# A one-core kernel of four attention and feed-forward layers, run from a new table of step times

## The chip, the core and the metric

The kernel runs on one core of one Trainium2 chip. Its time is the device time of one execution in microseconds (us). Before the change three runs took 1153.56, 1161.57 and 1164.41 us; the median is 1161.57 us.

The core has a matrix engine (PE, with its weight loads shown apart as PEld), VectorE (DVE), ScalarE (ACT), GpSimd (POOL), and the queue of SyncE (SP), which issues nearly all the DMAs. Each engine runs its own list of instructions strictly in order and waits on semaphores for what the others make.

## What is computed

x is 8 batches of 256 tokens by 256 features, ctx is as large, and a mask is given for one layer. Cut to its core, with L = 0 to 3:

```python
x = x + L0_xattn(layernorm(x), ctx)        # 16 heads of 16, strictly causal
x = x + L0_ffn(layernorm(x))               # x @ sign(W)
x = x + L1_xattn(layernorm(x), ctx)        # causal
x = x + L1_ffn(layernorm(x))               # 16 routed experts, top 2, and 2 shared ones
x = x + L2_xattn(ctx, layernorm(x), mask)  # q, k and v are normalised too
x = x + L2_ffn(layernorm(x))               # ternary weights, activations rounded to 8 bits
x = x + L3_xattn(layernorm(x), ctx)        # no projections
x = x + L3_ffn(layernorm(x))               # 3 blocks of dequantised plus low-rank products
```

The ternary weights of layer 2 are scaled by the mean of their absolute values, so those weights (six pieces of 512 KB) are read once for the sum and once more for the rounding.

## The kernel before

The kernel is one long program for each engine. Work is cut into steps, and each step is a method that exists on one engine or on several. An item is (L, b), the attention of layer L for batch b; there are 32 items, and `ORDER` (line 74) fixes their sequence, which the change keeps. An item has 16 heads in 4 groups. For each head PE makes the scores for the row maximum (`maxima`), DVE reduces them (`reduce`), PE makes the scores again with the maximum taken off (`score`), ACT takes the exponential (`exp`), and for each group PE multiplies with the values (`values`).

Around the attention stand other steps. `ln` on DVE takes the moments of a layer norm, `ln_power` on POOL the inverse root, `apply` on ACT the normalised rows, `turn` and `turned` the transposed copy. `k_stack` and `q_stack` on SP write the bf16 parts of keys and queries, six DMAs each, into the layout that `maxima` reads. `project_in`, `projected` and `project_out` are the output projection. `fill` (12 DMAs on SP, 10 of 768 KB and 2 of 128 KB) presets the DRAM rows of the experts. `raw_load(c)` on SP reads one of six pieces of the ternary weights into the buffer that `mask_load` uses too, and `raw_sum(c)` on DVE sums it; `raw_load(c)` waits for `raw_sum(c-1)`, and `raw_load(0)` waits for `masks(1)`. `scatter` and `fetch` are POOL's indirect DMAs of the routed tokens, and `gather`, `tile_load`, `tile_up`, `tile_down`, `tile_store` handle one of 62 tiles of 128 routed rows, with its expert's weights, in rings of four buffers.

What sets the order is the table `AT` (line 115). Each of 378 lanes is a generator of steps that depend on each other, and `AT` holds for each lane the times of its steps, 5,036 in all, in tenths of a us. `program` (line 1202) sorts all these times and calls the steps in that order. So a time in the table is no wait: it fixes only the place of the step in the lists of its engines, SP's and POOL's among them. Correct results rest on semaphores alone. The same clock also picks the PSUM bank of a product (`claim`), out of the banks that the table takes to be free.

Before the program starts, SP issues nine DMAs: keys' input and x for batch 0, three weights, two small tables, then the same two inputs for batch 1.

`wait_score` (line 2589) makes POOL wait, before each of its 64 indirect DMAs, for the score that the table has last before it.

Of the kernel before, what the change touches and what calls it, by code (L numbers as in the profile page):

```python
# [8 lines left out]
ALU = mybir.AluOpType  # L9
# [89 lines left out]
class Signal:  # L99
# [8 lines left out]

    def at(self, key):

        return self.sem, self.unit * (self.known.get(key, 0) + 1)
# [3007 lines left out]
```

## Time and profile before

| | before |
|---|---|
| median of three runs | 1161.57 us |
| profiled execution, first to last instruction | 1166.1 us |
| PE busy | 1050.5 us, 90% of the span |
| DVE, ACT, POOL busy | 903.8, 804.5, 564.1 us |
| granted PE clock, mean | 0.970 |
| DMA moved | 140.03 MB |

The profiled execution's own time is its span of 1166.1 us; no other time was taken of it. In the profile a busy PE includes time in which it ran at the lower clock. Steps are recognised by line and tile: line 2010 is `exp`, 2247, 2255 and 2259 are `reduce`, 1580 is `maxima`, 1598 is `score`, 1688 is `values`, 2136 is `ln`, 2890 is a stack DMA, 2942 is `fill`, 2983 is `raw_load`, 2403 is `raw_sum`, 2935 is `mask_load` and 2194 is `masks`.

### The profile page before, as it was taken

To read this page: it belongs to the slowest core of one execution; us is meant where nothing else is said; L and a number is where in the kernel's file an instruction comes from. 1 tells how busy PE (TensorE), PEld (TensorE's weight loads), DVE (VectorE), ACT (ScalarE), POOL (GpSimd) and SP (SyncE) were. 2 spreads that over 40 slices of the span, in tenths; PEclk is the share of its full clock that TensorE was granted. 3 is DMA by queue.
4 is the path that set the end of the run, shared out by engine and by line. 5 is a ranking of instruction groups with operands and counts; after the bars stand their busy time and mean duration, and the time that the engine had idled before them with its cause. 6 is when DMAs were issued, how large, how long until landed. Compare 5 with 4: busy or idle time off the path is not lost.

```text
span 1166.1 us, 26103 instructions
## 1 busy us (share of the span) xinstructions
PE 1050.5 (90%) x8259; PEld 782.0 (67%) x8298; DVE 903.8 (78%) x3323; ACT 804.5 (69%) x1484; POOL 564.1 (48%) x1161
## 2 busy tenths in 40 slices
PE   7989999999999989898888898788898989989986
PEld 6667877777887866676666765556665665656664
DVE  3879887877564688898885588999997889887643
ACT  5757666566674555566565667656989899998962
POOL 7232364655122365577830125766455454545443
PEclk9999999999999998999999999979999999999997
DMA  7985322325667643412258864232132222222000
GB/s 239 312 284 143 92 74 56 91 74 173 203 181 210 200 127 82 136 47 84 81 185 262 249 184 147 84 92 76 39 100 73 73 55 56 83 64 55 1 19 19
DMA packets 102327, 140.03 MB, mean 120 GB/s; under 512 B 12336, under 2 KB 79792, under 8 KB 102192
## 3 DMA queue, kind: packets, MB, share of 16 engines
q1 hardware_dynamic: 98688, 129.57, 38.0%
q0 software_dynamic: 3072, 8.39, 2.3%
q8 instruction: 69, 1.13, 0.4%
q14 instruction: 66, 0.54, 0.1%
q10 hardware_dynamic: 432, 0.39, 0.1%
HBM read 65.43 MB, written 22.54 MB: 75 GB/s over the span
## 4 chain that ended last, share of the span: by engine, by line
PE 40%; DVE 18%; ACT 15%; DMA 8%; issue 7%; SPq 5%; POOL 5%; another core or an unknown queue 1%; DVEq 0%; POOLq 0%; ACTq 0%
PE ps L1559 9%; PE ps L1688 4%; ACT probs L2010 4%; PE ps L1580 4%; PE ps L1598 4%; SPq L2890 3%; PE ps L1781 3%; PE ps L1552 3%; PE ps L1566 2%; ACT q_st L2027 2%; DVE ps L2247 2%; DMA w<-in_expert 2%; PE ps L1601 2%; DVE ps L2255 2%; PE ps L1748 1%
## 5 line engine op out<-in xcount | busy, mean ns | idle before, releaser
L2010 ACT ACTIVATE probs<-ps 128x384 f32<-128x384 f32 (+1 forms) x512 | 260.2, 545 | 91.4 <-PE ps L1601 46.4
L1580 PE MATMUL ps<-k_st,q_st 96*128 96x256 bf16 (+1 forms) x1024 | 172.4, 266 | 26.8 <-DVE neg_max L2247 10.3
L1598 PE MATMUL ps<-q_st,k_st 104*128 104x256 bf16 (+1 forms) x1024 | 178.0, 263 | 16.8 <-ACT probs L2010 12.3
L2027 ACT ACTIVATE q_st<-ps 8x1024 bf16<-8x1024 f32 x128 | 129.9, 1016 | 24.4 <-PE ps L1669 21.8
L1580 PEld LDWEIGHTS ps<-k_st,q_st 96*128 96x128 bf16 x1024 | 86.8, 100 | 79.1 <-DVE neg_max L2247 19.1
L2247 DVE CUSTOM_DVE_ANT_0 ps<-ps,diag_s 128x128 f32<-128x128 f32 (+1 forms) x384 | 123.3, 358 | 20.9 <-PE ps L1580 18.7
L1598 PEld LDWEIGHTS ps<-q_st,k_st 104*128 104x128 bf16 x1024 | 90.7, 99 | 61.7 <-issue 19.5
L1688 PE MATMUL ps<-probs,v 128*32 128x256 f32 (+1 forms) x2048 | 126.0, 365 | 2.0 <-ACT probs L2010 1.9
L2576 POOL TENSOR_SCALAR var_eps<-mv 128x2 f32<-128x2 f32 (+1 forms) x115 | 27.8, 242 | 185.2 <-DVE mv L2139 180.1
L2255 DVE CUSTOM_DVE_ANT_0 ps<-ps,mask_s 128x256 f32<-128x256 f32 x256 | 101.4, 452 | 6.2 <-PE ps L1580 5.8
L2658 POOL CAST parts<-qf 128x512 bf16<-128x512 f32 x64 | 40.5, 633 | 100.3 <-DVE qf L2166 44.7
L1688 PEld LDWEIGHTS ps<-probs,v 128*32 128x32 f32 x2048 | 55.0, 110 | 49.9 <-issue 25.8
L2259 DVE TENSOR_REDUCE neg_max<-ps 128x2 f32<-128x512 f32 x128 | 82.5, 680 | 5.4 <-PE ps L1580 2.9
L2581 POOL TENSOR_TENSOR rstd<-var_eps,neg_half 128x2 f32<-128x2 f32 (+1 forms) x115 | 84.4, 734 | 0.6
L2660 POOL TENSOR_TENSOR parts<-qf,parts 128x512 bf16<-128x512 f32 x64 | 75.0, 1173 | 5.2
L1559 PE MATMUL ps<-w,xn_t 128*128 128x256 f32 x296 | 74.1, 394 | 1.8 <-ACT xn_t L1906 1.2
L1959 ACT ACTIVATE xn<-x,shift,rstd 128x256 f32<-128x256 f32 x112 | 64.0, 633 | 16.2 <-POOL shift L2586 12.1
L1781 PE MATMUL ps<-ring,w 128*128 128x128 f32 x496 | 67.1, 281 | 6.5 <-DMA w<-in_expert 4.0
L2247 DVE DVE_READ_ACCUMULATOR2_ANT neg_max<- 128x1 f32 x512 | 72.5, 142 | 0.0
L1601 PE MATMUL ps<-diag_t,ident_b 128*128 128x256 bf16 x256 | 71.0, 278 | 0.0
L1781 PEld LDWEIGHTS ps<-ring,w 128*128 128x128 f32 x496 | 61.6, 193 | 12.1 <-issue 7.6
L1559 PEld LDWEIGHTS ps<-w,xn_t 128*128 128x128 f32 x296 | 54.7, 195 | 13.5 <-issue 6.8
(275 smaller groups left out, 2548.9 us busy)
## 6 DMA issues: line engine op xcount, KB each, us to landing
k_st<-parts SPq DMA_DIRECT2D x192, 128.0 KB
q_st<-parts SPq DMA_DIRECT2D x189, 128.0 KB, 2.8
w<-in_expert SPq DMA_DIRECT2D x62, 384.0 KB, 4.2
x_rows<-wo SPq DMA_DIRECT2D x10, 768.0 KB, 10.9
ctx_t<-in_ctx_t SPq DMA_DIRECT2D x16, 256.0 KB, 3.0
ring<-x_rows SPq DMA_DIRECT2D x31, 128.0 KB, 3.3
y_rows<-ring SPq DMA_DIRECT2D x31, 128.0 KB, 3.7
xn_t<-x_rows SPq DMA_DIRECT2D x31, 128.0 KB, 4.0
```

The lines of the kernel that those rows point to most:

```text
L1559: last = mm(t[:, a * D:(a + 1) * D], act_t[:, kt, a * P:(a + 1) * P], weight[:, kt, :], start=kt == 0, stop=kt == KT - 1)
L1580: last = mm(t[:, c0:c0 + n], head(q_st, r, h, KROWS, j * P, P), head(k_st, r, h, KROWS, 0, n), start=j == 0 or not by_pe, stop=not by_pe, ...
L1598: last = mm(t[:, j * S:j * S + n], head(k_st, r, h, KALL, j * P, P), head(q_st, r, h, KALL, skip, n), start=j == 0 or L == 3, stop=L == 3, ...
L1601: last = mm(t.rearrange("p (j t) -> p j t", j=SJ)[:, :, 0:P], ident_b[:, :], diag_t[:, L, :, :], start=False, stop=True, skip_group_check= ...
L1688: last = mm(t[h4 * DPAD:(h4 + 1) * DPAD, skip:S], v[:, r, j, hg * HPG + h4, :], probs[:, (hg % 2) * HPG + h4, j * S:(j + 1) * S - skip], s ...
L1781: last = mm(t[:, n * P:(n + 1) * P], expert[:, i % RING, c0:c0 + INNER_E], x_tile_t[:, i % 2, kt * P:(kt + 1) * P], start=kt == 0, stop=kt ...
L2010: nc.scalar.activation(probs[:, (hg % 2) * HPG + h4, 0:width], tile_of(key)[:, 0:width], ACT.Exp, scale=SCALE).then_inc(*tile_drained(key))
L2027: nc.scalar.activation(out, tile_of(key)[KROWS:KALL, 0:S].unsqueeze(1).to_broadcast([2 * HPG, HPG, S]), ACT.Copy).then_inc(*tile_drained(key))
L2247: last = V.tensor_tensor_reduce(some, some, diag_s[:, n0:n0 + j * step + 1:step, :], -1.0, -NEG, ALU.add, ALU.min, neg_max[:, hg, h4, j:j ...
L2255: last = V.tensor_tensor_reduce(some, some, mask_s[:, b % 2, j, :], -1.0, -NEG, ALU.add, ALU.min, neg_max[:, hg, h4, j:j + 1])
L2259: V.tensor_reduce(neg_max[:, hg, h4, :], tile_of(key).rearrange("p (j t) -> p j t", j=SJ), AX.X, ALU.max, negate=True).then_inc(*tile_drai ...
L2581: G.tensor_tensor(rstd[:, kind, tiles], var_eps[:, kind, tiles], neg_half[:, 0:SJ if a is None else 1], ALU.pow).then_inc(*ln_rstd.step((p ...
```

## The change

The table is replaced by another one with the same lanes and the same number of steps in each; its times are in hundredths of a us. No step changes its engine. `wait_score` goes. `sum_inv` gets two halves. Waits are written out where a buffer is used again: in `projected`, `quantised_copy`, `down_copy`, `normalise`, `load_batch` and `tile_load`.

```diff
@@ AT, first lines of four lanes (scores, fills, early, constants)
-    (287, 292, 303, 305, 322, 325, 339, 342, 370, 373, 386, 391, 416, 419, 432, 435, 456, 459, 470, 473, 496, 498, 509, 512,
...
-    (307, 313, 319, 336, 342, 348, 516, 543, 549, 555, 561, 567),
-    (168, 178, 184, 189, 195, 200, 205, 522),
-    (8, 65, 162, 219),
...
+    (3165, 3195, 3423, 3475, 3608, 3651, 3826, 3855, 3976, 4025, 4161, 4190, 4280, 4376, 4500, 4528, 5049, 5080, 5368, 5396,
...
+    (3322, 3366, 3405, 3444, 3483, 3522, 3561, 3600, 3639, 3678, 3717, 3756),
+    (1865, 1948, 2177, 2216, 2255, 2294, 2333, 2494),
+    (0, 866, 1624, 2382),
...
@@ program
-        clock[0] = t / 10
+        clock[0] = t / 100
@@ build
-        sum_inv = sb("sum_inv", [P, SJ, 2 * HPG])
+        sum_inv = sb("sum_inv", [P, 2, SJ, 2 * HPG])
@@ ACT
                 def projected(L, b):
+                    n = SLOT[L, b] - 1
+                    while n >= 0 and ORDER[n][0] == 3:
+                        n -= 1
+                    if n >= 0:
+                        wait_filled(act, ("wo", *ORDER[n]))
                     drain(("op", L, b), o_t[:, :, :])
                 def quantised_copy(b):
+                    if b:
+                        for T in range((b - 1) * SJ, b * SJ):
+                            for c in range(2):
+                                wait_filled(act, ("hu", T, c))
                 def down_copy(T):
+                    if T >= SJ:
+                        wait_filled(act, ("hd", T - SJ))
@@ DVE, normalise
+                    if SLOT[L, b]:
+                        wait_drained(dve, ("ot", *ORDER[SLOT[L, b] - 1], pair))
@@ POOL
-            def wait_score():
-
-                n = sum(10 * clock[0] > t for t in AT[0])
-                if n:
-                    L, b = ORDER[(n - 1) // H]
-                    wait_filled(pool, ("s", L, b, *divmod((n - 1) % H, HPG)))
...
-                    wait_score()
@@ SP, load_batch
-                if L == 0 and b >= 4:
-                    wait_filled(sp, ("v", 1, b - 4))
+                read = b - 4 if L == 0 else b + 4
+                if L == 0 and b >= 4 or L == 2 and b < 4:
+                    for what in ("k", "v"):
+                        for layer in range(2):
+                            wait_filled(sp, (what, layer, read))
@@ SP, tile_load
-                        wait_filled(sp, ("logit", LAST))
-                        wait_filled(sp, ("ed", LAST))
+                        for b in (B - 2, LAST):
+                            wait_filled(sp, ("logit", b))
+                            wait_filled(sp, ("ed", b))
```

Decoded with the lanes' generators, some entries of the two tables read as follows (us in the table, not measured):

| step | engine | before | after |
|---|---|---|---|
| load(0,3), inputs of batch 3 | SP | 22.0 | 0.0 |
| ln of batch 3 | DVE | 49.9 | 3.6 |
| ln of batch 0 | DVE | 3.7 | 4.5 |
| mask_load(0), masks(0) | SP, DVE | 32.5, 49.2 | 0.8, 5.4 |
| mask_load(1), masks(1) | SP, DVE | 53.2, 62.0 | 6.2, 10.1 |
| k_stack, q_stack of item (0,0) | SP | 10.1, 14.9 | 14.9, 19.9 |
| first maxima, first exp | PE, ACT | 19.9, 29.5 | 24.2, 33.6 |
| 12 fills | SP | 30.7 to 34.8 and 51.6 to 56.7 | 33.2 to 37.6 |
| raw_load(0), raw_sum(0) | SP, DVE | 62.9, 69.0 | 10.9, 15.6 |
| raw_load(1), raw_sum(1) | SP, DVE | 70.3, 77.7 | 24.5, 30.1 |
| raw_load(2), raw_sum(2) | SP, DVE | 80.1, 84.0 | 38.0, 43.2 |
| exp 49 of the 512 in sequence | ACT | 93.2 | 96.3 |
| exp 177 | ACT | 318.4 | 286.3 |
| last exp of layers 0 and 1 (exp 256) | ACT | 497.3 | 433.2 |
| exp 257 | ACT | 499.2 | 540.8 |
| exp 292, exp 293 | ACT | 580.9, 610.5 | 616.3, 616.8 |
| exp 353 | ACT | 763.0 | 729.8 |
| tile_load, first to last of tiles 0 to 30 | SP | 269.3 to 378.1 | 332.9 to 454.2 |
| tile_load, first to last of tiles 31 to 61 | SP | 563.1 to 633.1 | 490.2 to 580.9 |
| last exp | ACT | 1057.1 | 1032.1 |
| half_store(0), half_store(1), the last step | SP | 1106.5, 1107.5 | 1074.7, 1075.6 |

## Rows read from the trace of the kernel before

**Rows 1.** The page: span, busy time by engine, and PE's clock in 40 slices.

```profile
span 1166.1 us, 26103 instructions
PE 1050.5 (90%) x8259; PEld 782.0 (67%) x8298; DVE 903.8 (78%) x3323; ACT 804.5 (69%) x1484; POOL 564.1 (48%) x1161
PEclk9999999999999998999999999979999999999997
```

**Rows 2.** Busy time in six stretches: us, engines with counts, clock, DMA share, GB/s.

```profile
0.00:80.00 80.00, 65.89 (x517) 51.34 (x518) 51.61 (x240) 50.09 (x85) 34.77 (x82) 0.95 0.92 292
80.00:320.00 240.00, 230.76 (x2031) 184.39 (x2030) 189.82 (x909) 155.97 (x308) 111.09 (x258) 0.99 0.39 113
320.00:560.00 240.00, 218.82 (x1733) 174.09 (x1738) 181.67 (x759) 144.13 (x305) 125.30 (x261) 0.96 0.46 134
560.00:800.00 240.00, 208.50 (x1531) 148.17 (x1550) 194.46 (x633) 151.12 (x299) 107.27 (x194) 0.96 0.52 154
800.00:1120.00 320.00, 291.78 (x2306) 197.94 (x2320) 265.86 (x733) 288.58 (x458) 164.16 (x330) 0.99 0.22 61
```

**Rows 3.** Line 2010 alone in stretches from 0: ACT busy (count), clock, DMA.

```profile
0.00:102.80 102.80, 21.22 (x48) 0.95 0.82 257
0.00:332.40 332.40, 79.51 (x176) 0.98 0.53 160
0.00:527.20 527.20, 115.81 (x256) 0.97 0.51 151
0.00:817.90 817.90, 171.72 (x353) 0.96 0.51 149
```

**Rows 4.** The same for the stretch in which no exponential starts.

```profile
0.00:615.90 615.90, 135.75 (x292) 0.97 0.50 147
0.00:647.50 647.50, 136.24 (x292) 0.97 0.51 152
```

**Rows 5.** Timeline of SP at the end: start, us, what.

```profile
1162.23 2.04 SPq L3018 DMA_DIRECT2D out<-x  x2
```

**Rows 6.** Timeline of SP, DVE and ACT at the start, idle before in brackets.

```profile
4.56 0.66 SPq L2854 DMA_DIRECT2D x<-in_x  x1
4.20 0.75 DVE L2136 BATCH_NORM_STATS2 bn<-x 128x6 f32<-128x256 f32 x2 [4.20 <-DMA x<-in_x]
11.29 0.75 DVE L2136 BATCH_NORM_STATS2 bn<-x 128x6 f32<-128x256 f32 x2 [0.59 <-DMA x<-in_x]
21.90 0.30 DVE L2247 CUSTOM_DVE_ANT_0 ps<-ps,diag_s 128x128 f32<-128x128 f32 x1 [1.51 <-PE ps L1580]
32.42 1.02 ACT L2010 ACTIVATE probs<-ps 128x384 f32<-128x384 f32 x2 [1.48 <-PE ps L1601]
```

**Rows 7.** Timeline of SP, DVE and PE around the first `raw_load`.

```profile
58.85 3.55 SPq L2942 DMA_DIRECT2D x_rows<-wo  x5
68.35 0.33 SPq L2983 DMA_DIRECT2D mask_raw<-in_wq_gate  x1
77.54 1.22 DVE L2403 TENSOR_REDUCE wsum<-mask_raw 128x1 f32<-128x1024 f32 x1 [4.32 <-DMA mask_raw<-in_wq_gate]
79.53 0.87 PE L1566 MATMUL ps<-ident,o_tok 128*128 128x128 f32 x3 [4.22 <-DVE o_tok L2285]
```

**Rows 8.** DMA issues: name, count, KB each, median us from issue to landing.

```profile
x_rows<-wo SPq DMA_DIRECT2D x10, 768.0 KB, 10.9
...
mask_raw<-in_wq_up SPq DMA_DIRECT2D x4, 512.0 KB, 3.7
```

**Rows 9.** The stretch of the first six fills: columns as in rows 2.

```profile
33.60:51.80 18.20, 16.74 (x182) 12.57 (x181) 14.91 (x83) 14.39 (x26) 3.53 (x4) 0.97 1.02 342
```

**Rows 10.** Waits: who waited for whom, us in total, times, longest.

```profile
ACT o_t L1906 <- PE ps L1566: 8.9, 4, 4.6
SPq L2864 <- PE ps L1559: 11.9, 3, 8.2
POOL ring L2816 <- PE ps L1601: 5.1, 3, 1.8
POOL xn_t L2816 <- PE ps L1598: 4.2, 3, 2.2
```

More of the change, by code:

```diff
@@ L107, in step, with drain @@
         return self.sem, self.unit
+    def drain(self, key):
+        return self.sem, self.unit
     def at(self, key):
@@ L1429, in tile_drained @@
             new_drain_at[key] = clock[0] + DRAIN
-            return drained[bank_of[key]].sem, 1
+            return drained[bank_of[key]].drain(key)
         def wait_filled(eng, key):
@@ L2280, in normalise @@
                     wait_filled(dve, key)
+                    if SLOT[L, b]:
+                        wait_drained(dve, ("ot", *ORDER[SLOT[L, b] - 1], pair))
+                    inv = sum_inv[:, pair, :, :]
                     t = tile_of(key).rearrange("p (a h e) -> p a h e", a=SJ, e=DPAD)
-                    V.reciprocal(sum_inv[:, :, :], t[:, :, :, DH]).then_inc(*inverted.step((L, b, pair)))
+                    V.reciprocal(inv, t[:, :, :, DH]).then_inc(*inverted.step((L, b, pair)))
                     dve.wait_ge(*inverted.at((L, b, pair)))
                     out = o_tok[:, r, :, pair * 2 * HPG * DH:(pair + 1) * 2 * HPG * DH].rearrange("p a (h d) -> p a h d", d=DH)
-                    V.tensor_tensor(out, t[:, :, :, 0:DH], sum_inv[:, :, :].unsqueeze(3).to_broadcast([P, SJ, 2 * HPG, DH]), ALU.mult).then_inc(
+                    V.tensor_tensor(out, t[:, :, :, 0:DH], inv.unsqueeze(3).to_broadcast([P, SJ, 2 * HPG, DH]), ALU.mult).then_inc(
                         *tile_drained(key))
@@ L2814, in fetch @@
                             pool.wait_ge(*y_out[i % RING].at(i))
-                    wait_score()
                     G.indirect_dma_start(y_in(b, n), None, y_rows[g],
@@ L2856, in load_batch @@
             def load_batch(L, b):
-                if L == 0 and b >= 4:
-                    wait_filled(sp, ("v", 1, b - 4))
+                read = b - 4 if L == 0 else b + 4
[3 more added lines that the diff above has]
+                            wait_filled(sp, (what, layer, read))
                 if L == 2:
-                    if b < 4:
-                        wait_filled(sp, ("v", 1, b + 4))
-                    else:
+                    if b >= 4:
+                        for what in ("k", "v"):
+                            wait_filled(sp, (what, 2, b - 4))
                         sp.wait_ge(*part_rest.at(("k", 3, b - 4)))
```

1077 rows, old and new, of the table AT are left out of this document.

## The prediction

> **What bounds the kernel now.** I read the page first. PE is busy for 1050.5 of 1166.1 us [rows 1], so no order of the same steps can save more than PE's idle 115.6 us and what the lower clock costs. The mean granted clock of 0.970 puts that at 0.03 x 1166.1 = 35 us or less. By stretch [rows 2] the idle time is 14.1 of the first 80 us, 9.2 of the next 240, 31.5 of the 240 from 560 and 28.2 of the 320 from 800. DVE is the second engine, busy for 194.5 of 240 us from 560 to 800.
>
> Then I asked how well the old table foretold the run. The exponentials can be counted: 48 have run at 102.8 us, 176 at 332.4, 256 at 527.2 and 352 (the count of 353 has one table load in it) at 817.9 [rows 3]; the next one starts at once in each case. The old table puts these at 93.2, 318.4, 499.2 and 763.0. So the run is behind its table by 9.6, 14.0, 28.0 and 54.9 us, and by 55.7 at half_store(0), which starts at 1162.23 for a table time of 1106.5 [rows 5]. The last 350 us add under 1 us: there the table is as good as a measurement. What the table misses is 2.9 us at the first exponential against 29.5 in the table [rows 6], 6.7 up to 102.8, and 46 between 102.8 and 1162.
>
> **The sum's frame.** The new table's last step stands at 1075.6, the old one's at 1107.5. The span ends at 1166.1, that is 2.9 us after table time plus 55.7. So the new span is 1075.6 + 2.9 + lag = 1078.5 + lag, and the question is the lag. I take a table time for nothing but this: a place from which measured lateness is counted.
>
> **Lag at the start: 7 us.** DVE's first step becomes the ln of batch 3, whose x is now the eleventh DMA. The ninth is issued at 4.56 and lands at 11.29, with DVE waiting for it [rows 6]; two more of 256 KB behind it, 0.9 us each at the 292 GB/s of the first 80 us [rows 2], put this one at about 13. Before, DVE began at 4.20. Behind stand the ln of batch 0, masks(0), only then SP's mask_load(1), which takes 3 us or more (512 KB take 3.7, [rows 8]), masks(1) and then the first k_rest: about 20 us. POOL, from the ln of batch 0 at 15, has some 13 us of steps in its list up to the end of q_low of item (0,0), and q_stack lands 3 us later, near 31. The table wants the first maxima at 24.2: 7 us late, against 2.9 before. Bounds: 4 and 10.
>
> **Lag from the raw sums: 21 us.** This is the largest cost. The 12 fills (7.9 MiB, 8.1 MB) stood in two lots of six; now they stand in one row on SP, and raw_load(2) is right behind them. The trace of before has this in small: raw_load(0), issued at 68.35 behind the second lot, reached DVE at 77.54, 9.2 us against 3.7 for a lone one [rows 7, 8]. DVE idled 4.32 us, PE then 4.22, since only two PSUM banks hold maxima [rows 7]. Transfers land nearly in the order of issue: a fill takes 10.9 us in the median [rows 8]. In the new list SP has, from 28 us on, 4.5 MB of weights and inputs, two stacks of 0.8 MB and then the fills. The first part, 6.1 MB, lands by about 49 us at 292 GB/s. The fills need 8.1 MB at 342 GB/s [rows 9] = 24 us, or 19 at the 430 that a stretch of pure fills might reach (my upper guess). raw_load(2), 1.5 us behind them, then lands between 69.5 and 74.5, and raw_sum(2) ends 1.2 us later [rows 7]. The table ends it at 44.4. So the lag is 26 to 31 there, and I take 28. raw_sum(1), also behind 2 MB of weights, is a step of 2 us on the way and is contained in it. Behind raw_sum(2) on DVE stand normalise of (0,0) and all row maxima; behind raw_load(3) on SP, which waits for raw_sum(2), stand the stacks of item (0,2). PE is planned nearly without gaps from there to 433, so little of it is won back. Bounds for the whole start: 10 (no more than before had) and 33 (two us on top of the upper value).
>
> **Lag from 100 us on: 23 us.** Before it was 46. Part of that was a table that priced PE's steps too low: with each kind of PE step at the distance which the table usually leaves to the next step (a third up the sorted distances), the old table's PE steps sum to 967 us and the new one's to 993. Those 26 us of work are already in the new table's 1075.6, so they no longer come as lag. The other 20 are lower clock (at most 30 of the 35 us lie behind 102.8) and late transfers; I keep them. The long stall at the start adds 3: after its 4.22 us stall PE's clock was down for a while [rows 7], and the mean of the first 80 us is 0.95 [rows 2]. Bounds: 8 (a denser PE keeps its clock) and 46 (everything comes again).
>
> **The edits in code: 0.** The new waits name work that PE has long done in either table: the wo before a project_in, hu before quantised, hd by 20.9 us or more before the next down_turn. Their cover is PE's own order. ACT's wait in projected was 8.9 us in all and is for the turn that follows wo [rows 10]. The wait in normalise is for DVE's own earlier step; without cover each costs one semaphore turn. SP's waits in load_batch name k and v of layers 0 and 1; the latest of them is v of layer 1, which it waited for before (11.9 us, [rows 10]). wait_score held POOL 5.1 and 4.2 us in front of two groups of fetches [rows 10]; nothing late hangs on them now, so its removal gains 0, at best 5.
>
> **Sum.** 28 + 23 = 51; span 1078.5 + 51 = 1129.5 us. The profiled execution lies 4.5 us above the median of 1161.57, so I forecast 1125 us, 3.1% less. Where the gain would come from is PE's idle time between 320 and 800 and after; where it is lost is the first 80 us.
>
> **Rival A, the front costs little.** If a late transfer does not have to wait for those issued before it, raw_load(2) lands 4 to 5 us after issue and the early lag is 11: 1078.5 + 11 + 23 - 4.5 = 1108. Against it stand the 9.2 us of rows 7; for it, that the same DMA engines serve all. With the later bound of 8 it would be 1093. The Trainium skill (DMA: Bandwidth & Descriptors, section Queues, rings and completion order) says of transfers of one issuing engine that completion is not in the order of issue, only the start on each DMA engine. By that sentence's first half alone this rival would hold, by its second the forecast does; the 9.2 us agree with the second. Chance 0.2.
>
> **Rival B, the gain is eaten.** The later lag comes in full: 28 + 46 = 74, and the table has a stretch of 107.6 us without exponentials (433.2 to 540.8), in which tiles, ternary weights and layer 2's projections must fill PE. Before, such a stretch of 29.6 us in the table (580.9 to 610.5) took 31.8 [rows 4], 7% more; that is 8 us here. Sum 1078.5 + 82 - 4.5 = 1156. For it: DVE, at 194.5 of 240 us, is packed tighter in the new table between 560 and 800. Against: the last 350 us of before, where DVE was as dense (265.9 of 320, [rows 2]) and nothing was lost. Chance 0.19.
>
> **Rival C, slower.** The queue at the front is the mechanism, at a higher price. With the 54 us of rival B's later part, 1173 (1% more than before) is reached at an early lag of 45. That needs the fills and what stands before them to drain in 15 us more than at 342 GB/s, so at about 210, and raw_load(3) and the stacks of (0,2) late by as much. At an early lag of 50 it is 1178 us. The first stretch moved 292 GB/s in the mean [rows 2], which speaks against. Chance 0.09.
>
> **Numbers.** Forecast case 0.52, A 0.2, B 0.19, C 0.09. About 1% is what a measurement of this kernel can tell from no change (its three runs lie 0.9% apart). Faster by over 1% (below 1150): the forecast case, A and a fifth of B, 0.75. Within 1%: 0.16. Slower: 0.09. The range: 1078.5 + 10 + 8 - 4.5 = 1092 below and, with both upper bounds, 1078.5 + 33 + 46 - 4.5 = 1153 above; I take 1094 to 1160, to hold half of B above its sum too.
>
> **What would show it.** DVE's first moments at 12 to 13 us and not 4; the first exponential at 40 us (3 either way); one idle stretch of DVE in front of its third line 2403 of 10 us or more, ended by the DMA of the raw weights, and PE idle behind it; exponential 49 at about 124 us; from there on a lag that grows by 20 to 25 us to the end. PE's idle time from 320 to 800 falls from the 52.7 us of before to some 25. If exponential 49 comes before 110, the front is priced too high; if the lag after it grows by over 40, the second half is where I am wrong.

## The result and the profile after

The changed kernel takes 1167.54 us (median of 16 runs, 1163.5 to 1172.4), the kernel before 1160.58 beside it (16 runs). The ratio is 1.0062, 95% interval 1.0040 to 1.0085: 7 us or 0.6% slower. I had forecast 1125 us, faster by 3.1%, with a range that ended at 1160; the kernel lies above it. The outcome within 1% of before had been given a chance of 0.16.

The page of the kernel after, for [rows 1]:

```profile
span 1167.5 us, 26206 instructions
...
PE 1041.5 (89%) x8298; PEld 783.1 (67%) x8298; DVE 899.4 (77%) x3323; ACT 805.8 (69%) x1486; POOL 561.6 (48%) x1161
...
PEclk7779999999999899999999998999999999999998
```

Busy time of every engine is within 1% of before. PE's idle time grew from 115.6 to 126.0 us. The three slices of 7 at the left of the clock row are new. The stretches of [rows 2], after:

```profile
0.00:80.00 80.00, 41.45 (x264) 31.81 (x264) 30.04 (x118) 31.01 (x49) 29.94 (x71) 0.79 0.79 270
80.00:320.00 240.00, 230.36 (x2062) 180.39 (x2062) 194.26 (x961) 160.82 (x306) 95.61 (x197) 0.98 0.32 90
320.00:560.00 240.00, 225.88 (x1835) 188.99 (x1835) 167.72 (x735) 134.66 (x306) 119.11 (x311) 0.98 0.54 165
560.00:800.00 240.00, 214.83 (x1607) 153.73 (x1608) 206.03 (x699) 168.95 (x329) 133.40 (x223) 0.96 0.55 157
```

Both halves of the result are in these rows. In the first 80 us PE did 264 matmuls where it did 517 before, and idled for 38.5 us instead of 14.1. From 320 to 800 it idles for 14.1 + 25.2 = 39.3 us instead of 52.7. A gain stands behind, a loss in front.

The count of exponentials (line 2038 now), for [rows 3]; 48 have run when the next one starts at 133.8, 176 at 328.1, 256 at 601.5:

```profile
0.00:133.70 133.70, 21.43 (x48) 0.85 0.62 203
0.00:328.00 328.00, 79.13 (x176) 0.94 0.43 132
0.00:486.80 486.80, 114.89 (x256) 0.95 0.46 142
0.00:601.40 601.40, 115.38 (x256) 0.95 0.51 155
```

The new table has these at 96.2 (96.25, rounded up in the table of steps), 286.3 and 540.8, so the run is 37.6, 41.8 and 60.7 us behind it, and 89.0 at half_store(0), which starts at 1163.71 for a table time of 1074.7 (for [rows 5]):

```profile
1163.71 2.04 SPq L3055 DMA_DIRECT2D out<-x  x2
```

Exponential 49 is the best place to cut the run, since nearly the same work lies in front of it in both tables (408 of 423 steps are the same). Columns as in [rows 2], first the kernel before, then after, each with its part up to exponential 49 and its tail:

```profile
0.00:102.90 102.90, 88.47 (x716) 68.85 (x717) 72.09 (x324) 66.13 (x115) 43.95 (x97) 0.95 0.82 256
102.90:1166.10 1063.20, 962.06 (x7546) 713.13 (x7583) 831.71 (x3001) 738.33 (x1371) 520.19 (x1064) 0.97 0.37 107
```

```profile
0.00:133.80 133.80, 90.71 (x698) 69.32 (x698) 74.71 (x333) 64.88 (x112) 44.76 (x97) 0.85 0.62 203
133.80:1167.50 1033.70, 950.84 (x7600) 713.77 (x7600) 824.67 (x2991) 740.94 (x1375) 516.88 (x1064) 0.98 0.38 109
```

The front became 30.9 us longer, of which 28.7 is PE idle time (43.1 against 14.4). The tail became 29.5 us shorter: 18.2 less idle, 11.2 less busy, the latter with the clock at 0.98 instead of 0.97. The old table's tail is 1014.3 us and the new one's 979.4, a promise of 34.9.

What fills the front, timelines of SP, PE, ACT and DVE of the kernel after (for [rows 6, 7]):

```profile
13.35 0.75 DVE L2175 BATCH_NORM_STATS2 bn<-x 128x6 f32<-128x256 f32 x2 [13.35 <-DMA x<-in_x]
38.04 0.80 PE L1608 MATMUL ps<-k_st,q_st 96*128 96x128 bf16 x4 [5.15 <-DMA q_st<-parts]
40.33 3.81 SPq L2926 DMA_DIRECT2D k_st<-parts  x6
55.61 0.60 ACT L1976 ACTIVATE parts<-ps 128x512 bf16<-128x512 f32 x1 [8.85 <-issue]
56.10 0.87 ACT L2038 ACTIVATE probs<-ps 128x384 f32<-128x384 f32 x2
49.92 10.52 SPq L2978 DMA_DIRECT2D x_rows<-wo  x12
60.48 19.22 SPq L3020 DMA_DIRECT2D mask_raw<-in_wq_up  x2
78.13 1.22 DVE L2445 TENSOR_REDUCE wsum<-mask_raw 128x1 f32<-128x1024 f32 x1 [11.73 <-DMA mask_raw<-in_wq_up]
80.67 1.13 PE L1608 MATMUL ps<-k_st,q_st 96*128 96x128 bf16 x4 [10.08 <-DVE neg_max L2286]
```

Two stalls are in these rows. The first exponential waits on ACT behind `k_hi` of item (0,2) (line 1976), which idles ACT for 8.85 us; by the code it waits until the stack DMAs of item (0,1) have landed, and these were issued from 40.33 on, behind the weights. The profile names no releaser here (`<-issue`). The other thing that the step waits for, POOL's splits of item (0,1), had ended by 43.1, so the stacks are what is left; the trace of e4_front below names them. The second is the forecast one: `raw_load(2)` issued at 60.48 right behind twelve fills, landed for 78.13, DVE idle for 11.73 us and PE for 10.08 behind it.

### The profile page after: what moved, and what is told of

Its sections match the earlier page's. It is cut to its first block, busy times and chain, and to the rows that moved or that the text cites. A ratio compares the mean times of both kernels' runs of the same rounds, so it can differ in the third digit from the quotient of the medians.

```text
span 1167.5 us, 26206 instructions
## 1 busy us (share of the span) xinstructions
PE 1041.5 (89%) x8298; PEld 783.1 (67%) x8298; DVE 899.4 (77%) x3323; ACT 805.8 (69%) x1486; POOL 561.6 (48%) x1161
## 4 chain that ended last, share of the span: by engine, by line
PE 45%; DVE 27%; ACT 8%; DMA 6%; SPq 6%; issue 6%; POOL 2%; DVEq 0%; another core or an unknown queue 0%; POOLq 0%; ACTq 0%
PE ps L1587 10%; PE ps L1716 5%; PE ps L1608 4%; PE ps L1626 4%; DVE ps L2294 4%; PE ps L1809 4%; PE ps L1580 3%; DVE ps L2286 3%; DVE bn L2175 3%; SPq L2926 3%; PE ps L1594 3%; ACT probs L2038 2%; DMA mask_raw<-in_wq_up 2%; DVE neg_max L2298 2%; PE ps L1816 2%
## 5 line engine op out<-in xcount | busy, mean ns | idle before, releaser
L2618 POOL TENSOR_SCALAR var_eps<-mv 128x2 f32<-128x2 f32 (+1 forms) x115 | 28.8, 250 | 216.9 <-DVE mv L2178 211.0
L2693 POOL CAST parts<-qf 128x512 bf16<-128x512 f32 x64 | 39.7, 621 | 119.9 <-DVE qf L2205 52.7
L1716 PEld LDWEIGHTS ps<-probs,v 128*32 128x32 f32 x2048 | 54.5, 110 | 48.8 <-issue 24.2
L1587 PE MATMUL ps<-w,xn_t 128*128 128x256 f32 x296 | 71.6, 385 | 3.6 <-ACT xn_t L1934 1.3
L1809 PEld LDWEIGHTS ps<-ring,w 128*128 128x128 f32 x496 | 64.9, 199 | 9.2 <-issue 4.5
L1587 PE MATMUL ps<-w,ctx_t 128*128 128x256 f32 x256 | 64.1, 395 | 0.2 <-DVE ring L2515 0.2
```

What stands on the lines that cost most here:

```text
L1587: last = mm(t[:, a * D:(a + 1) * D], act_t[:, kt, a * P:(a + 1) * P], weight[:, kt, :], start=kt == 0, stop=kt == KT - 1)
L1716: last = mm(t[h4 * DPAD:(h4 + 1) * DPAD, skip:S], v[:, r, j, hg * HPG + h4, :], probs[:, (hg % 2) * HPG + h4, j * S:(j + 1) * S - skip], s ...
L1809: last = mm(t[:, n * P:(n + 1) * P], expert[:, i % RING, c0:c0 + INNER_E], x_tile_t[:, i % 2, kt * P:(kt + 1) * P], start=kt == 0, stop=kt ...
```

## The experiments

All times below are medians, and ratios are to the kernel before, run beside each; its own median was 1157.14 to 1161.10 us from one set of runs to the next, so different runs are compared by their ratios. Exponential 49 and spans come from each run's profiled execution. Steps are named and given their table times in us.

**The code edits alone (e1_edits).** The old table in the new code.

```diff
-AT = (new table)
+AT = (old table, each time x 10)
```

> The old table (times multiplied by ten, so the same order) in the new code. My theory, the forecast's: the code edits cost 0, so 1160 us, within 0.3% of before, and exponential 49 at 102.8 us. Rival: the new waits are part of the 50 us by which the new kernel falls behind its table after 134 us; then this kernel is slower than before, by 5 to 27 us, and by the same stretch it lags the old table by more than 55 us at the end.

Measured: 1153.54 us, ratio 0.9975 (0.9947 to 1.0003). The edits cost nothing that can be measured. Its profiled execution taught more:

```profile
0.00:105.00 105.00, 88.80 (x715) 69.19 (x716) 72.98 (x324) 66.05 (x114) 43.70 (x97) 0.95 0.80 251
105.00:1146.60 1041.60, 948.94 (x7546) 704.86 (x7583) 830.06 (x3001) 739.39 (x1371) 521.00 (x1064) 0.99 0.38 109
```

The same order and the same work as before has a tail of 1041.6 us here and of 1063.2 in the execution that I had read. 13.1 of the 21.6 are PE busy time, at a clock of 0.99 against 0.97. The old table has 1014.3 us for the tail, so its later lag, 48.9 us by span in the execution that I had read (the forecast's 46 counts to half_store(0)), is 27.3 in this one.

That this execution is quick is not the edits' doing: at 1148.37 us it is the quickest of its twelve (1148.37 to 1159.73). The 35 executions of the kernel before that ran beside it spread by 16 us, and with the clock: those with a mean granted clock of 0.984 took 1147.94 and 1149.71 us, those with 0.971 took 1157.23, 1161.43 and 1163.56. A profiled execution at 0.970, as I had read, and one at 0.984, as here, are near the two ends.

**Raw sums later (e2_raws), batch 3 later (e3_ln3), the whole front as before (e4_front).** All three on the new kernel:

```diff
 # e2_raws
-raw_load(2..5) 38.0 44.5 53.4 65.3   raw_sum(2..5) 43.2 49.1 64.0 70.0   raw_total 90.6   round_load(0) 101.3
+raw_load(2..5) 62.0 72.3 83.0 100.4  raw_sum(2..5) 68.5 77.9 91.2 111.1  raw_total 157.9  round_load(0) 165.0
 # e3_ln3
-load(0,3) 0.0   ln 3.6   ln_power 4.7   apply 29.3  turn 32.2  turned 38.6
+load(0,3) 23.4  ln 49.9  ln_power 51.0  apply 54.8  turn 60.2  turned 61.1
 # e4_front: e3_ln3 and
-masks(0), masks(1) 5.4 10.1   fill(0..11) 33.2 .. 37.6                raw_load(0) 10.9
+masks(0), masks(1) 49.2 62.0  fill(0..5) 30.7 ..  fill(6..11) 51.6 ..  raw_load(0) 62.9
   (the other raw loads and sums at 70.3 .. 111.1, raw_total 157.9, round_load(0) 165.0)
```

> The new kernel, but pieces 2 to 5 of the raw weights are loaded and summed later (table times 62 to 111 us instead of 38 to 70; sum of all and first round load behind them). Fills and everything else stay. Theory: the 11.7 us for which DVE stood in front of raw_sum(2) go, the first exponential stays at 56 us, exponential 49 comes about 12 us earlier (121 to 123 us), and the whole is about 1155 us. Rival: the queue of 12 fills itself is the cost, because the stacks of item (0,2) and their rows stand behind it as well; then exponential 49 stays within 3 us of 133.8 and the time within 3 us of 1167.

> The new kernel, but batch 3's input is loaded and normalised later, at the old table's place (load at 23.4, ln at 49.9, its later steps behind). Theory: DVE starts at 4 us and not at 13.4, the first exponential comes 6 to 9 us earlier (47 to 50 us), raw_sum(2) by the same 6 to 9, and the whole is 1159 to 1162. Rival: the masks and the raw weights ahead of the first stack hold the start as well; then the first exponential moves by under 3 us and the time stays within 3 us of 1167.

> The new kernel, but batch 3's load and ln, both masks, all fills, all raw loads and sums and the total are put at the old table's places (fills in two lots again). Theory: the front alone costs 28 us, PE is packed from there on and gives nothing back; exponential 49 at 106 to 110 us instead of 133.8 and the whole at 1137 to 1144 us, faster than both kernels. Rival: the early lateness is slack that a later wait would have used anyway (the tiles, the 108 us without exponentials); then exponential 49 comes early as well, but the lag after it grows by 65 to 78 instead of 50 and the time stays above 1155.

| | exponential 1 | exponential 49 | ratio to before |
|---|---|---|---|
| after | 56.1 | 133.8 | 1.0062 (1.0040 to 1.0085) |
| e2_raws | 55.8 | 127.5 | 1.0033 (1.0005 to 1.0061) |
| e3_ln3 | 49.2 | 126.9 | 1.0045 (1.0019 to 1.0071) |
| e4_front | 43.7 | 114.7 | 0.9956 (0.9928 to 0.9983) |

Each step moves exponential 49 in the direction foretold. e3_ln3 met its numbers for the front (DVE starts at 4.14, and the third raw sum, at 71.69, is 6.4 us earlier), e2_raws gave half (6.3 us for 12), between its two expectations. For the whole both had been expected to give more: 1.0033 and 1.0045 are 1164 and 1165 us beside a before of 1160, foretold were 1155 and 1159 to 1162. Alone they are worth 0.2 to 0.3% with intervals that overlap those of the kernel after; only both together, with masks and fills, make it faster than before. e4_front was 8 to 15 us slower than foretold by its median of 1151.67 us, 11 to 18 by its ratio, and the chain of waits of that run up to its first exponential shows why:

```profile
31.80 11.34 DMA k_st<-parts
43.21 0.60 ACT parts L1799
43.81 0.39 ACT probs L1861
```

The last of the k stack DMAs of item (0,1) took 11.34 us to land, with the weights issued in front of it, and `k_hi(0,2)` stands in front of the first exponential in the new table (31.8 against 33.6), while the old one has it 6.4 us behind.

**That wait alone (e7_khi).** e4_front with the splits of item (0,2) moved behind the first exponentials.

```diff
-k_hi(0,2) 31.8  q_hi(0,2) 36.3  (k_rest, k_low, q_rest, q_low 37.1 to 39.8)
+k_hi(0,2) 42.0  q_hi(0,2) 45.0  (k_rest, k_low, q_rest, q_low 43.0 to 46.5; q_stack 45.8 -> 48.6)
```

> The kernel with all of the front moved (e4_front), and beside that ScalarE's k_hi and q_hi of item (0,2) with the split steps behind them stand 9 to 10 us later in the table, behind the first exponentials. Theory: in e4_front k_hi(0,2) stands in front of the first exponential and waits 11.3 us for the stack DMAs of item (0,1), which are behind 3 MB of weights; the first exponential comes at 33 to 37 us instead of 43.7, exponential 49 at 106 to 110 instead of 114.7, and the time is 5 to 8 us less than e4_front's 1151.7. Rival: the maxima of the next groups need the same stacks; then the first exponential comes early, but exponential 49 stays within 2 us of 114.7 and so does the time.

Measured: 1149.87 us, ratio 0.9901 (0.9869 to 0.9934); first exponential at 36.97, no longer behind a DMA, exponential 49 at 110.0. The 4.7 us came through in the trace; the ratio moved by 0.55% (6 us), with intervals that overlap a little. The rival said exponential 49 would stay, and it did not.

**The fills alone (e9_fills).** The new kernel, only the fills moved.

```diff
-fill(0..11) 33.2 .. 37.6 (0.4 apart)
+fill(0..11) 85.0 .. 178.5 (8.5 apart)
```

> The new kernel, but the 12 fills alone are moved, from the table times 33 to 38 us to 85 to 179 us, one at a time. Masks, batch 3 and all raw loads and sums stay where the new table has them. Theory: raw_sum(2) came 35 us late because 8.1 MB of fills stand right in front of its load; without them it comes at 58 to 64 us instead of 78.1, exponential 49 at 116 to 121 us instead of 133.8, and the time is 13 to 18 us less than the new kernel's 1167.5. Rival: the weights and stacks in front hold the raw load as much; then raw_sum(2) comes after 70 us and the time is within 6 us of 1167.5.

Measured: 1155.21 us, ratio 0.9956 (0.9934 to 0.9977), so 12.3 us less than after, just under the foretold 13 to 18. The third raw sum, DVE timeline:

```profile
66.65 1.21 DVE L2268 TENSOR_REDUCE wsum<-mask_raw 128x1 f32<-128x1024 f32 x1
```

It starts at 66.65, not 78.13 (foretold 58 to 64), and waits for no DMA. Exponential 49 comes at 122.3 instead of 133.8 (foretold 116 to 121), and what was gained by then (11.5 us) is there at the end. The first exponential stays at 55.4: that stall is not the fills'. This one move of twelve instructions is worth more than the whole loss of the change.

**Old front, new tail, and the reverse (e5_oldfront, e6_newfront).** In the new code, the 423 steps up to exponential 49 in one table's order, all others in the other's.

```diff
 # e5_oldfront: time of a step
-T_new
+T_old + 3.0 if T_old < 93.2 else T_new   (the 15 only the new front has: 96 to 114 us; raw_total 157.9, raw_scale 162, round_load(0) 165)
 # e6_newfront
+T_new if T_new < 96.2 else T_old + 3.0   (the 15 only the old front has: 96.2 to 97.2 us)
```

> The new code and the new table, but the first 423 steps (all up to exponential 49) stand in the old table's order; the ten steps that only the new table has in that part follow directly behind. Theory: front and tail add. The old front puts exponential 49 at 103 to 106 us, the new tail from there takes its 1034 us, so 1135 to 1140 us, 2% less than before. Rival: the tail was quick only because everything behind the long stall was ready (weights, fills, stacks); then the tail takes 1045 to 1060 us and the time is above 1148.

> The reverse: the new table's order up to exponential 49, the old table's order behind it. Theory: exponential 49 at 132 to 135 us and the old tail of 1045 to 1063 us, so 1180 to 1195 us, slower than both kernels by 2%. Rival: the old tail takes up part of the lateness, since its table leaves PE more idle time; then the time is 1160 to 1175.

e5_oldfront: 1147.99 us, ratio 0.9883 (0.9860 to 0.9906). e6_newfront: 1211.06 us, ratio 1.0429 (1.0407 to 1.0451). The two profiles, cut at exponential 49:

```profile
0.00:105.00 105.00, 88.85 (x716) 69.73 (x717) 72.13 (x324) 66.14 (x114) 43.71 (x97) 0.93 0.78 251
105.00:1145.10 1040.10, 947.42 (x7545) 709.76 (x7583) 827.86 (x3001) 740.97 (x1373) 516.86 (x1064) 0.98 0.38 109
```

```profile
0.00:132.80 132.80, 89.84 (x700) 68.48 (x701) 75.06 (x333) 65.19 (x112) 44.77 (x97) 0.86 0.64 205
132.80:1206.00 1073.20, 963.59 (x7561) 713.79 (x7598) 827.39 (x2991) 740.79 (x1373) 520.61 (x1064) 0.97 0.36 105
```

The first measures the new order behind exponential 49: 1.17% or 13.6 us better than the old one, with the old front. The new front then costs 1.0062 - 0.9883 = 1.8% or 21 us, of 28.8 us that exponential 49 comes later: the tail behind the long stall is 1033.7 us and that behind the short front 1040.1. So 6 to 8 us seem to come back, as the rival had it in kind but not in size; the ratios are sure to some 4 us, and the tails are of one execution each, so this is likely and not shown. It would account for most of the 8 us by which e5_oldfront missed my 1140. The reverse, above both expectations, is spoilt by its seam: item (1,0), its steps squeezed together with the 15 that had been put off, took 32 us for 15 exponentials where the kernel before took 17. With these 15 us taken off, some 35 of its 50 us are left for the new front with the old tail; no more than that can be read from it.

**Fills and raw sums spread (e8_spread).** On e5_oldfront.

```diff
-fill(0..11) in two lots at 34 and 55 to 60   raw_sum(0..5) 72 .. 114
+fill(0..11) 42.0 .. 168.5, 11.5 apart        raw_sum(0..5) 92 .. 212, 24 apart
   (raw_load(0..5) 12 in front of each sum; raw_total 232, raw_scale 236, round_load(0) 240)
```

> e5_oldfront with the 12 fills spread over the table times 42 to 169 us and the raw loads and sums over 80 to 212 us, each alone on the queue. Theory: what is left of the front's lateness (9.7 us at exponential 49, most of it behind raw sums and fills) is the queue again; exponential 49 at 99 to 102 us and the time 2 to 5 us under e5_oldfront's. Rival: no transfer is late in the old front any more and the rest is PE and DVE work; then it is within 1 us of e5_oldfront, or 1 to 3 us slower, since raw sums now stand in the dense part of DVE.

Measured: 1140.49 us, ratio 0.9819 (0.9796 to 0.9843). This beats both kernels: 1.8% under before and, by 0.9819 / 1.0062, 2.4% under after. It gains 0.64% on e5_oldfront, 7.4 us, more than foretold:

```profile
0.00:99.70 99.70, 86.92 (x716) 67.78 (x717) 70.34 (x325) 66.17 (x114) 44.18 (x97) 0.97 0.69 209
99.70:1137.80 1038.10, 944.95 (x7545) 710.40 (x7583) 828.59 (x2999) 741.23 (x1373) 516.92 (x1064) 0.98 0.39 115
```

5.3 us of it lie in front of exponential 49. Fills and raw pieces moved together here, so their shares are not known.

**What the tail is short of (e10_dve2, e11_dve01, e12_half).** On e8_spread, in `reduce` on DVE:

```diff
 # e10_dve2 (condition L == 2), e11_dve01 (L < 2 and not one of the first three items)
+                    if L == 2:
+                        V.tensor_reduce(probe[:, h:h + 1], diag_s[:, 0:2, :].rearrange("p n k -> p (n k)"), AX.X, ALU.max)
                     wait_filled(dve, key)
 # e12_half
-   tile_of(key).rearrange("p (j t) -> p j t", j=SJ),
+   tile_of(key).rearrange("p (j t) -> p j t", j=SJ)[:, :, 0:P],
```

> e8_spread with one more VectorE reduction (128x256 bf16, a result that nothing reads) in front of each of layer 2's 128 row maxima: 128 of some 0.3 us, about 40 us of DVE between 570 and 980 us. It asks what the new tail is short of. Theory: there PE waits mostly for DVE, which is busy 209 of 231 us from 569 on, so this costs over half of what it adds, 20 us or more. Rival: PE alone sets the pace and DVE has room; then it costs under 8 us.

> e8_spread with the same reduction in front of the 208 row maxima of layers 0 and 1 from item (1,0) on: 208 of some 0.3 us, about 65 us of DVE between 97 and 460 us. Theory: DVE is busy for only 349 of 469 us from exponential 49 to layer 2, so PE sets the pace and this costs under 15 us. Rival: only two PSUM banks hold maxima, so each us before a reduce is a us for PE whatever DVE's idle time; then it costs 30 us or more.

> e8_spread, but layer 3's 128 row maxima on VectorE are taken over only half of the keys (128x256 instead of 128x512, 0.68 us each in e8_spread; the maximum is then not the true one, the rest of the work is as before). That takes some 0.27 us off each, 35 us of DVE in all, after 720 us. Theory: the added reductions passed on three quarters of their DVE time to the whole, so the tail is short of DVE as much as of PE, and taking time away gives back half or more: 15 to 26 us less than e8_spread. Rival: PE's idle time there is of other origin and DVE was only just in time; added DVE work costs, removed work gains under 6 us.

| | DVE busy | time | ratio to before | against e8_spread |
|---|---|---|---|---|
| e8_spread | 898.9 | 1140.49 | 0.9819 (0.9796 to 0.9843) | |
| e10_dve2 | 933.0 | 1166.98 | 1.0057 (1.0031 to 1.0082) | +34.1 busy, +2.4%, 27.6 us |
| e11_dve01 | 955.7 | 1179.24 | 1.0174 (1.0144 to 1.0204) | +56.8 busy, +3.6%, 41 us |
| e12_half | 868.9 | 1131.26 | 0.9744 (0.9708 to 0.9780) | -30.0 busy, -0.8%, 9 us |

(Last column: difference of the ratios x 1160 us; by the intervals of the ratios each is sure to 4 or 5 us.) The added reduction stands in front of the wait for PE's scores, so it could have filled time in which DVE waits. Added DVE time still comes through at 81% and 73%. For e10_dve2 that is my theory. For e11_dve01 it is the rival's side: I had said under 15 us, because DVE was idle for a quarter of that stretch, and it cost 41. Less DVE time gave back 30% (9 us, 4 to 14 by the intervals), between the two expectations. The profiled execution of e12_half, the slowest of its six, has a span of 1137.8 us, the same as that of e8_spread; in it DVE's waits for PE in front of the shortened maxima grew from 10.6 to 21.8 us. PE's waits in the stretch of layer 2, first in e8_spread (570 to 960 us), then in e10_dve2 (570 to 980): us in total, times, longest.

```profile
PE ps L1431 <- DVE neg_max L2121: 4.4, 4, 3.2
PE ps L1431 <- DVE neg_max L2117: 4.3, 8, 1.4
PE ps L1449 <- ACT probs L1861: 4.1, 3, 2.3
```

```profile
PE ps L1432 <- DVE neg_max L2120: 15.2, 31, 1.7
PE ps L1521 <- DVE max_parts L2137: 6.2, 13, 1.9
```

Eight waits of half a us in front of the maxima (L1431, L1432) become 31. Of the 27.4 us by which the span grew, 16.8 are PE idle time and 10.6 PE busy time (1042.5 against 1031.9), at a granted clock of 0.976 against 0.981. My reading is that PE, DVE and the two banks between them run in step: a delay of either is felt, a relief of one only until the other is next. It is not shown, because time was added in layers 0 to 2 and taken away in layer 3, and no run did both to the same layer.

## Why the prediction was wrong, step by step

My forecast put exponential 49 at 124 us and the tail at 1129.5 - 124.2 = 1005.3 us. They are 133.8 and 1033.7. So of the 42.5 us between 1125 and 1167.54, 9.6 are the front and 28.4 the tail. The remaining 4.5 are what I took off because the execution I had read lay above its median; the new kernel's profiled span, 1167.5, is its median.

**The front's place and mechanism: right, and too small.** DVE's first moments came at 13.35 (12 to 13 foretold) and the idle stretch of 10 us or more before the third raw sum was there (11.73), with PE idle behind it. e9_fills shows the fills as the cause of 11.5 us of it.

**"Lag at the start: 7 us": failed.** It was 22.5, the first exponential at 56.1 and not 40. I had walked DVE's and POOL's lists up to the first maxima and put these at 31; they came at 38.04, after a wait for q_st. ACT's list I had not walked. There `k_hi(0,2)` waits for DMAs issued from 40.33 to 44 behind the weights; it idled ACT for 8.85 us, and e7_khi shows 6.7 us for its place in e4_front. Batch 3's load and ln, which I did price, are worth 6.9 us at the first exponential (e3_ln3). For the sum only the part counts that makes SP's list late, because the landing of raw_load(2) holds DVE whenever the first exponential comes. Batch 3 is such a part: with it moved SP issues its load of batch 2 at 23.55 and not at 30.88, and its 6.9 us are there at exponential 49 too (e3_ln3). When the fills are gone, 26.0 us of lag are left at exponential 49 (e9_fills).

**"Lag from the raw sums: 21 us", to 28 in all: mis-sized.** raw_sum(2) ended at 79.35 where I had 72.4, and 2.7 us more were lost up to exponential 49; the 37.6 are 4.6 over my upper bound of 33. The rate was right:

```profile
30.00:78.10 48.10, 25.44 (x202) 17.86 (x200) 20.61 (x93) 25.87 (x41) 14.63 (x18) 0.82 0.95 336
```

336 GB/s over the whole queue, where I had 292 for its first part and 342 for the fills. But the weights went out from 30.88 and not from 28: a queue that is full hands its late start on, 2.9 of the 7.0 us. Most of the other 4 are a miscount of bytes: by the sizes of its DMAs, SP's list from 30.88 up to raw_load(2) holds 15.9 MB and not 14.7. The weights, inputs and first stack in it are 5.6 MB where I had 4.5, and 1.2 MB at 336 GB/s are 3.4 us.

**"Lag from 100 us on: 23 us": failed, the largest error.** It was 1033.7 - 979.4 = 54.3 by span, against 1063.2 - 1014.3 = 48.9 before. The credit of 26 us for a table that prices PE's steps higher was an artefact. Distances between neighbours in a table are, as I now read them, work plus the gap that the planner leaves, so a sum of them is no price of the work. The two rows of each tail tell: PE is busy for 962.1 us in the old tail, 950.8 in the new one, the same work within 1.2% (948.9 in e1_edits' tail, which makes it 0.2%), so the old table's 1014.3 left PE some 52 us idle and the new one's 979.4 some 29, and the real idle time was 101.1 and 82.9. These two executions idle PE by about 50 us more than their tables say. Nor is that a constant of the kernel: the later lag is 49 to 61 us in the eight profiled executions that have the new tail (after, e2, e3, e4, e5, e7, e8, e9), and 27.3 and 48.9 in the two that have the old one. The new table's lag is the larger one, where I had made it the smaller. Rival B had this part nearly right: 46 + 8 = 54, against 51.4 counted to half_store(0). PE's idle time from 320 to 800 fell by 13.4 us, to 39.3, and not to some 25.

Within it, the 8 us for the stretch without exponentials measured 7.1 (a lag of 53.6 at 486.8 us, 60.7 at 601.5). The rest grew in small pieces, from 328 to 487 and from 602 to 839 most. Another 10 came behind 839 (a lag of 78.6 at exponential 370, 89.0 at half_store(0)); from exponential 370 on the old table's had stood still (55.2 to 55.7), and I had called a table as good as a measurement there. That DVE is part of its cause e10_dve2 and e11_dve01 show; how much of the 50 us is DVE's, the lower clock's or transfers' is open, and e12_half speaks against DVE as the whole. The step that failed is known, the cause of the lag itself stays open.

**The old lag of 46 was itself one draw.** The same order had 27.3 against 48.9 in e1_edits. I had one execution, at a granted clock of 0.970, and took it as the kernel's.

**The code edits: 0, right** (ratio 0.9975, an interval that holds 1).

**Rival C, slower, is what the sum came near,** from below and with rival B on the other side (1167.5 between 1156 and 1173): it asked for an early lag of 45 and a later one of 54; the later was there (51.4 at half_store(0)) and the early one was 37.6, which gives slower by 0.6% and not by 1%. I had called it unlikely because it needed 210 GB/s. It came near with no low rate at all, by a later lag that I had credited away. **Rival A** fell: raw_load(2) landed 17.6 us after its issue. The Trainium skill (DMA: Bandwidth & Descriptors, Queues, rings and completion order) says that each DMA engine takes turns between the queues for which it has work. The three q stack DMAs that ACT issued on its own queue at 27.93 landed in 2.5 us in the median, but SP's queue was nearly empty then, so no run here shows whether another queue would have spared the stacks the 11.34 us.

## What to carry to other kernels

Bulk transfers with no reader for 100 us (fills, second copies of weights) belong one by one between the urgent ones, never in a row in front of them: spreading the fills gave 12 us here in the bad order, and fills and raw pieces together 7 in the good one. When an order is judged, walk the list of every engine up to the first useful step, ask of each step that waits for a DMA what was queued ahead of that DMA, and start a queue's count at the real time of its first issue. And compare two plans by measured busy time at the same milestones; a lag read from one execution here was uncertain by 20 us, and its mean granted clock hints at which end it lies.

## What the runs showed of the hardware

An idle front goes with a lower clock. Up to exponential 49 the granted clock is 0.85 after, with PE idle for 43.1 us, and 0.95 before, with 14.4; both are a mix of its levels of 1.2 and 2.4 GHz. PE is busy for 2.2 us more there than before, for 18 matmuls fewer. In the stretch in which ACT waited for the stack and PE with it, the granted clock was 0.70, with PE busy for 1.06 of 7.0 us:

```profile
50.70:57.70 7.00, 1.06 (x7) 0.80 (x8) 0.12 (x2) 2.07 (x4) 0.00 (x0) 0.70 1.10 309
```

I had not expected that DVE work would come through to the time at 73% (e11_dve01) in a stretch where DVE is busy for only three quarters: 349 of 469 us in e8_spread.

```profile
99.70:569.00 469.30, 437.52 (x3666) 355.57 (x3665) 349.10 (x1588) 285.47 (x608) 230.32 (x532) 0.99 0.52 155
```

Average idle time said nothing about what stands in the loop between `maxima` and `reduce`.
